# Layer 1's two dense products by Strassen's scheme in a two-layer GraphSAGE kernel

## The reference

```python
def _sage_layer(h, edge_src, edge_dst, deg_inv, W_self, W_neigh, b):
    msg = h[edge_src]
    agg = jax.ops.segment_sum(msg, edge_dst, num_segments=h.shape[0])
    mean = agg * deg_inv[:, None]
    return h @ W_self + mean @ W_neigh + b
h   = jax.nn.relu(_sage_layer(x, src, dst, deg_inv, W_self0, W_neigh0, b0))
out = _sage_layer(h, src, dst, deg_inv, W_self1, W_neigh1, b1)
return _layernorm(x + out, axis=-1)        # x: 1250 x 1024
```

## Time and profile before

| | us |
|---|---|
| median of 3 runs | 683.05 (680.74 to 683.33) |
| the profiled execution, its own time | 681.76 |
| its span, first to last instruction | 680.1 |

### The profile page before, as it was taken

One profiled execution on the slowest core, in us unless ns is written; L12 is line 12 of the kernel. 1 busy time (PEld: TensorE's weight loads), 2 busy tenths in 40 slices (PEclk: granted clock), 3 DMA queues, 4 the chain that ended last, 5 costly groups with the idle time before them and its releaser, 6 DMA issues.

```text
span 680.1 us, 11592 instructions
## 1 busy us (share of the span) xinstructions
PE 646.3 (95%) x3404; PEld 335.0 (49%) x3404; DVE 383.0 (56%) x1003; ACT 198.4 (29%) x349; POOL 118.3 (17%) x194
## 2 busy tenths in 40 slices
PE   3778989998999999999999999999999999999995
PEld 3634545543666666555555444444444444444442
DVE  7796586868777877378889845241033322322223
ACT  5672724344344444213336401231100000000000
POOL 4001236632233333200000000000041111101100
PEclk9799989999999999999999999999999999999999
DMA  8614000000000000060000500000211011111100
GB/s 320 248 70 178 1 0 0 0 0 1 1 1 1 0 0 0 3 249 1 0 0 0 212 36 1 0 0 0 94 63 62 32 62 62 62 62 34 51 31 24
DMA packets 11393, 33.40 MB, mean 49 GB/s; under 512 B 1976, under 2 KB 2136, under 8 KB 11360
## 3 DMA queue, kind: packets, MB, share of 16 engines
q1 hardware_dynamic: 11360, 32.99, 13.2%
HBM read 27.87 MB, written 5.12 MB: 49 GB/s over the span
## 4 chain that ended last, share of the span: by engine, by line
PE 88%; DVE 4%; issue 3%; DMA 2%; ACT 1%; SPq 1%; POOL 0%; POOLq 0%; DVEq 0%; ACTq 0%
PE ps L539 26%; PE ps L653 15%; PE ps L566 15%; PE ps L674 13%; PE ps L605 12%; PE ps L463 5%; DMA ws<-in_L_gnn_W_neigh 2%; DVE wn L248 1%; PE ps L619 1%; SPq L284 1%; DVE xz L967 1%; PE ps L475 1%; DVE ws L248 1%; PE ps L491 1%; ACT ws L726 1%
## 5 line engine op out<-in xcount | busy, mean ns | idle before, releaser
L539 PE MATMUL ps<-wn,xz 128*128 128x512 f16 x480 | 116.5, 382 | 2.8 <-DVE wn L248 1.4
L566 PE MATMUL ps<-xz,ws 128*128 128x420 f16 (+1 forms) x576 | 116.1, 339 | 0.0
L653 PE MATMUL ps<-wn,zh 128*128 128x512 f16 x480 | 105.2, 379 | 0.0
L934 DVE TENSOR_SCALAR scratch<-iota_q,table 125x240 f16<-125x240 f16 x320 | 104.0, 325 | 0.3 <-issue 0.2
L539 PE MATMUL ps<-ws,zh 128*128 128x512 f16 x480 | 103.8, 379 | 0.0
L932 DVE TENSOR_SCALAR lohot<-iota_lo,table 125x128 f16<-125x128 f16 x320 | 87.6, 274 | 26.0 <-PE ps L463 25.2
L380 POOL TENSOR_TENSOR A<-A,scratch 128x120 int32 x160 | 72.6, 454 | 139.5 <-ACT scratch L699 111.5
L699 ACT ACTIVATE scratch<-ps 128x240 uint16<-128x240 f32 x160 | 58.9, 370 | 120.8 <-PE ps L463 102.8
L674 PE MATMUL ps<-xz,A 128*128 128x512 f16 x400 | 88.0, 379 | 0.0
L605 PE MATMUL ps<-A,zh 128*128 128x420 f16 (+1 forms) x480 | 84.7, 340 | 0.0
L653 PEld LDWEIGHTS ps<-wn,zh 128*128 (+1 forms) x480 | 46.9, 98 | 56.7 <-issue 0.2
(11 more groups left out here) (127 smaller groups left out, 432.4 us busy)
## 6 DMA issues: line engine op xcount, KB each, us to landing
ws<-in_L_gnn_W_neigh SPq DMA_DIRECT2D x8, 1024.0 KB, 12.9
zh<-in_x SPq DMA_DIRECT2D x9, 512.0 KB, 8.2
ws<-in_x SPq DMA_DIRECT2D x9, 512.0 KB, 3.2
out<-ws SPq DMA_DIRECT2D x18, 256.0 KB, 2.1
ws<-in_L_gnn_W_self SPq DMA_DIRECT2D x4, 1024.0 KB, 8.7
wn<-in_L_gnn_W_self SPq DMA_DIRECT2D x4, 1024.0 KB, 8.1
ws<-in_L_gnn_b SPq DMA_DIRECT2D x1, 512.0 KB, 3.8
zh<-in_x SPq DMA_DIRECT2D x1, 392.0 KB
```

Source lines behind the costliest of these rows:

```text
L539: ins = pe.matmul(ps[0:TP, 2 * r + half, :], lhs(a, k, t), w[:, k, b, half * HD:(half + 1) * HD], start=(k == 0 and a == 0 and b == 0), st ...
L566: ins = pe.matmul(ps[:, b, 0:CH[n]], ws[:, k, a, bass.ds(f * P, P)], xT[h][:, k, CO[n]:CO[n] + CH[n]], start=(k == 0 and a == 0 and h == 0 ...
L653: ins = pe.matmul(ps[0:TP, g + half, :], zh[:, k, a, bass.ds(t * TP, TP)], wn[:, k, b, half * HD:(half + 1) * HD], start=(k == 0 and a == ...
L934: ins = dve.tensor_scalar(qhot[0:EP, r, k, :], iota_q[0:EP, :], q[0:EP, b, bass.ds(row, 1)], None, ALU.is_equal)
```

## The change

Both dense products of layer 1 are computed by Strassen's scheme (Winograd's form). h is cut in two along the nodes (tile p and tile p+5) and in two along the features (k-tiles 0 to 3 and 4 to 7), the weights in two by two blocks. Each pair p of node tiles then takes seven products m of 12 matmuls of 512 columns (4 k-tiles x 3 splits), where the scheme before took 2 x 48: 35 products or 420 matmuls for each of `h Wn1` and `h Ws1`, not 480.

- h is kept in fp32 (`H`), and no longer split as a whole. Before each product an *item* is made: ACT writes the high part of its operand into a ring of 8 slots, DVE the low part, seven products ahead. Products 5, 6, 3 and 7 of each pair need a sum of two blocks of h, which POOL makes (`s_sum`, chained: each waits for the one before).
- The weights are loaded in pieces, twice (once for their maximum, once for the factors). For each of four k the seven factors T are made: four by subtractions on POOL (`t_sum4`), high parts on ACT, low parts on DVE (28 of each per product stage).
- In the first product stage three products of each pair (1, 5, 6) are copied from PSUM by ACT (`kept`), three (2, 3, 7) are added to such a copy by DVE (`c_made`), and four results of 512 columns are split into z1. In the last one DVE adds each of the 35 products to y in SBUF.
- The two branches of layer 1 are turned round: the first product stage (`h Wn1`), then all ten tiles of `A z1`, whose results with x and b1 added are spilled to DRAM for eight of the ten tiles and read back, then the second product stage (`h Ws1`) with the layer norm in it.
- All of this is written out, where it was in loops.

The core of the diff:

```diff
+    ORDER7 = [(0, 1)]
+    for pair in range(IT):
+        last = pair == IT - 1
+        ORDER7 += [(pair, m) for m in ((5, 6, 3, 7, 2) if last else (2, 5, 6, 3, 7))]
+        ORDER7 += [(pair, 4)] if last else [(pair + 1, 1), (pair, 4)]
...
@@ POOL
             spread(2)
+            for k in range(HK):
+                t_sum4(0, k)
             pool.wait_ge(unit_ready, 3 * (KT - 1))
-            pool.memset(zh[:, 0:KT, :, N:NP], 0.0).then_inc(h_tail_zero, 1)
+            for k in range(KT):
+                ins = pool.memset(H[k][:, N:NP], 0.0)
+            ins.then_inc(h_tail_zero, 1)
+            pool.wait_ge(h32_ready, 3 * KT)
+            for i in range(4):
+                s_sum(i)
             spread(3)
+            for i in range(4, 4 * IT):
+                s_sum(i)
+            pool.wait_ge(b1_in, 16)
+            for n in range(4):
+                residual(n)
             spread(4)
-            pool.wait_ge(b1_in, 16)
-            with pool.Fori(0, IT) as i:
-                residual(i)
+            pool.wait_ge(item_low, NP7)
+            for k in range(HK):
+                residual(4 + k)
+                t_sum4(1, k)
...
+            for i in range(4 * IT, 8 * IT):
+                s_sum(i)
@@ PE
+            def product(phase, e):
+                p, m = ORDER7[e]
+                b = 3 * (p % 2) + {1: 0, 6: 0, 7: 0, 4: 0, 2: 1, 5: 2, 3: 2}[m]
+                pe.wait_ge(item_low, NP7 * phase + e + 1)
+                if phase == 0:
+                    if m == 1 and p >= 2:
+                        pe.wait_ge(z_low, 4 * (p - 1))
+                    if m in (6, 3, 7):
+                        pe.wait_ge(kept_ready, KEEP7.index((p, {6: 1, 3: 5, 7: 6}[m])) + 1)
+                    if m == 4:
+                        pe.wait_ge(c_made, MADE3.index((p, 7)) + 1)
+                else:
+                    if m == 1 and p >= 2:
+                        pe.wait_ge(y_acc, AT7[p - 2, 4] + 1)
+                    if m in (6, 3, 7, 4):
+                        pe.wait_ge(y_acc, AT7[p, {6: 1, 3: 5, 7: 6, 4: 7}[m]] + 1)
...
+                for k in range(HK):
                     for a, bs in ((0, (0, 1)), (1, (0,))):
+                        for w in bs:
+                            ins = pe.matmul(ps[:, b, :], slot[:, k, a, :], Tm[m][:, k, w, :], ...)
...
@@ ACT, first product stage
+            for e in range(1, ITEMS):
+                item(0, e)
+            for e in range(NP7):
+                p, m = ORDER7[e]
+                if e + ITEMS < NP7:
+                    item(0, e + ITEMS)
+                if m in (1, 5, 6):
+                    act.wait_ge(product_done, e + 1)
+                    if p:
+                        act.wait_ge(c_made, MADE3.index((p - 1, {1: 2, 5: 7, 6: 3}[m])) + 1)
+                    act.activation(kept[{1: 0, 5: 1, 6: 2}[m]], ..., ACT.Copy).then_inc(kept_ready, 1)
+                else:
+                    z_item(MADE7.index((p, m)))
@@ DVE, end of the neighbours and last product stage
+                    unit(f, n)
                     if 3 * f + n:
+                        hmax(*divmod(3 * f + n - 1, 3))
...
+            item_lows(0, 0)
+            hmax(KT - 1, 2)
...
+            for e in range(NP7):
+                p, m = ORDER7[e]
+                if e + ITEMS < NP7:
+                    item_lows(1, e + ITEMS)
...
+                dve.wait_ge(product_done, NP7 + e + 1)
+                dve.scalar_tensor_tensor(yh, ps[0:TP, 3 * (p % 2) + b, :], c("cs1", TP), yh,
+                                         ALU.mult, ALU.add).then_inc(y_acc, 1)
+                if m in (2, 3, 7, 4):
+                    dve.wait_ge(y_acc, e + 1)
+                    dve.bn_stats(st[0:TP, r, 6 * h:6 * h + 6], yh).then_inc(stat_ready, 1)
+                if m == (3 if p < IT - 1 else 2):
+                    finish(2 * p)
+                if m == 4:
+                    finish(2 * p + 1)
```

More of the change, by code:

```diff
@@ L324, in store_row @@
                     apart(sp)
-                    rows = LAST if isinstance(i, int) and 2 * i + r == JT - 1 else TP
-                    sp.dma_start(out[bass.ds((2 * i + r) * TP, rows), half], obuf[r][0:rows, half]).then_inc(o_stored[r], 16)
-            def tile_slices(t):
-                with sp.If(nwin > 1):
-                    load_slices(sp, TILES + t, t * TP, TP)
-            for r in range(2):
-                load_row(0, r, True)
-            for r in range(2):
-                tile_slices(r)
@@ L337, in _ @@
-            with sp.Fori(0, IT - 2) as i:
-                for r in range(2):
-                    load_row(i + 1, r)
-                    store_row(i, r)
-                    tile_slices(2 * i + 2 + r)
-            for r in range(2):
-                load_row(IT - 1, r)
-                store_row(IT - 2, r)
-                tile_slices(2 * IT - 2 + r)
-            for r in range(2):
-                store_row(IT - 1, r)
+                    sp.dma_start(out[t * TP:t * TP + rows, half], yrow(p, r)[0:rows, half]).then_inc(o_stored[r], 16)
@@ L662, in tile @@
+            for e in range(NP7):
+                product(0, e)
+            def tile(n, with_rest):
+                t = TILES_B[n]
+                g = 6 if n % 2 == 0 else 3
+                if n >= 2:
+                    pe.wait_ge(y_ready, 2 * n - 2)
+                elif n == 1 or with_rest:
+                    pe.wait_ge(z_low, 4 * IT)
+                if n == 0 and not with_rest:
+                    pe.wait_ge(z_low, 4 * (IT - 1))
                 if with_rest:
                     for j in range(JT):
-                        w = slice_in(pe, TILES + t, j)
+                        w = slice_in(pe, TILES + n, j)
@@ L840, in finish @@
+            act.wait_ge(scale_ready, 6)
+            for k in range(HK):
+                for i in range(ITEMS):
+                    t_item(1, k, i)
+            act.wait_ge(t_low, 2 * ITEMS * HK)
+            for e in range(ITEMS):
+                item(1, e)
+            def finish(n):
+                p, r = n // 2, n % 2
+                y = yrow(p, r)
+                act.wait_ge(var_ready, n + 1)
                 act.activation(ln[0:TP, r, 1:2], ln[0:TP, r, 0:1], ACT.Sqrt).then_inc(std_ready, 1)
-                act.wait_ge(shift_ready, t + 1)
@@ L842, in finish @@
-                if not first:
-                    act.wait_ge(o_stored[r], 32 * i)
-                act.activation(obuf[r][:, 0:HD], ybuf[r][:, 0:HD], ACT.Identity, bias=ln[0:TP, r, 3:4],
+                act.wait_ge(shift_ready, n + 1)
+                act.activation(y[:, 0:HD], y[:, 0:HD], ACT.Identity, bias=ln[0:TP, r, 3:4],
                                scale=ln[0:TP, r, 2:3]).then_inc(o_ready[0], 1)
-            finish(0, 0, True)
-            finish(0, 1, True)
-            with act.Fori(1, IT) as i:
-                for r in range(2):
-                    finish(i, r, False)
+            for e in range(NP7):
+                p, m = ORDER7[e]
+                if e + ITEMS < NP7:
+                    item(1, e + ITEMS)
+                if m == (3 if p < IT - 1 else 2):
+                    finish(2 * p)
+                if m == 4:
+                    finish(2 * p + 1)
@@ L1086, in _ @@
                 onehots(NG - GT + g, g, (NG - GT + g) // GR)
-            def groups(i, extra):
-                for r in range(2):
-                    if not (isinstance(i, int) and i == 0 and r == 0):
-                        low(2 * i + r - 1, 1 - r, 1)
-                    for m in range(2):
-                        extra(i, 2 * r + m)
             nwin = dve.value_load(nwin_i[0:1, 0:1], min_val=1, max_val=NWIN)
@@ new lines, in _, with z_low_part @@
+            for e in range(1, ITEMS):
+                item_lows(0, e)
+            def z_low_part(i):
+                p, m = MADE7[i]
+                t, half = p + (IT if m in (7, 4) else 0), slice(0, HD) if m in (2, 4) else slice(HD, D)
+                dve.wait_ge(z_high, i + 1)
+                dve.scalar_tensor_tensor(z1[1][:, t, half], ps[:, 3 * (p % 2), :] if m == 4 else
+                                         made[MADE3.index((p, m)) % 2], c("s_z1"), z1[0][:, t, half],
+                                         ALU.mult, ALU.subtract).then_inc(z_low, 1)
```

566 lines of the change are left out of this document (367 added, 199 removed).

## The result

The changed kernel took **703.66 us** (median of four runs, 702.37 to 704.27) beside 682.92 for the kernel before: a ratio of 1.0308, 95% interval 1.0281 to 1.0334. The forecast was 678 us, faster, with a range up to 690: wrong in sign, and outside its range. The profiled execution has a span of 702.2 us, against 680.1 before and 675.1 by the forecast's sum: 27.1 us are to be explained. Of the runs further down, e8 had two slow executions among its ten (840.53 and 1322.84 us): its median of 683.41 counts them, its ratio leaves them out.

A forecast was written before the change was run, and what follows sets the result against it. PE was taken to bound the kernel, busy 95% of the span. -25.9 + 2.4 + 10.4 + 1.5 + 4.2 + 0.9 + 1.5 = -5.0 us, so 683.05 - 5.0 = 678 us, range 665 to 690.

The forecast's parts named there:

- What it removes: Both dense products of layer 1: 60 of 480 matmuls fewer in each, at 0.2158 us, 25.9 us saved.
- Neighbours: Neighbours stage: DVE about 74 of 84.3 us, no loss taken; slack of 10 us as cover, up to 5 if POOL is late.
- Start of the first product: Start of first product stage: PE waits 2.4 us for item 0's low part, on DVE behind the last unit.
- The fifth sum: First product stage: POOL's fifth item sum, behind `spread(3)` and its two operation changes, makes PE wait 10.4 us.
- Clock: First product stage: granted clock 0.50 for 3 us, expected once, behind the long wait; 1.5 us lost.
- Tiles: Tiles stage: POOL 65.5 of 86.3 us, DVE about 47; nothing lost, up to 4 us if the POOL chain comes late.
- Last product: Last product stage: DVE's queue makes PE wait 0.4 and 0.8 us at products 3 and 4 of pairs; 4.2 us.
- POOL against DVE: DVE low parts slowed beside POOL's sums: 1.5 us taken, between nothing and 24 us for a stage.
- Rival 2: Last product stage bound by DVE, low parts waiting 0.4 us behind each of 20 sums; 6 to 7 us added, 685; chance 0.17.
- signs of being wrong: Layer 1: idle before the neighbours end, a last stage of over 100 us, or a long wait on the items themselves.

The follow-up runs named there:

- e8: e7 with the sixteen differences of the first factor (neighbours stage) on DVE too, so POOL reads nothing there; 683.41 us.
- e10: Changed kernel rearranged: no spread on POOL, factor differences and first four item sums on DVE, row maxima replaced by ACT's absolute sums, low parts four ahead; 667.40 us.
- e1: Changed kernel with each of POOL's 76 sums and differences replaced by three writes of a constant, sums left out of the computation; 25.5 us less.
- e9: e4 with each of POOL's 76 sums replaced by three writes of a constant, sums left out of the computation; 673.06 us.
- e4: e3 with the maxima of both second factors also spread off POOL, so POOL changes no operation in the part the change touches; 689.08 us.
- e3: Changed kernel with the maximum of h spread by a diagonal on DVE, a product with ones on PE and a DVE reduction, not on POOL; 6.8 us less.
- e2: e1 with one write of a constant in place of three, so POOL neither reads SBUF nor takes long; 10.4 us less than e1.
- e7: e6 with one maximum per row of h instead of three, and last-stage low parts after the running product's accumulation and statistics; 683.34 us.
- e5: Changed kernel with low parts of items 3 to 6 of the last product stage moved after the last tile's eviction on DVE; 703.48 us.
- e6: e4 with e5's move, and the first four item sums of each product stage made by DVE instead of POOL; 686.84 us.

## Why the prediction was wrong

- **What it removes, 25.9 us:** right. The last product of e10 takes 91.0 us for 420 matmuls.
- **Neighbours, "I take nothing":** wrong in the changed kernel, with the cover named (DVE's slack of 10 us), and right without the blocking: in e1 the stage and the wait behind it take 87.1 us, forecast 86.7. DVE's own work was estimated at 74 us; without blocking it is 77.9 to 80.9 (e1 over 84.7 us, e9), and blocking brings it to 89.3 of 92.6 in e4.
- **Start of the first product, 2.4 us:** the mechanism and size are right once nobody blocks DVE (2.44 in e1 and e9). With blocking it is 5.68.
- **The fifth sum, 10.4 us:** measured 10.24, in the place and with the two changes as forecast: 6.03 us of idle time ahead of the spread and 7.36 behind it, against 5.77 and 6.95 of the earlier trace rows. That the size fits so well is partly luck. Counted from the end of the neighbours (383.23), h was complete after 5.2 us and not after 2.1, and the fifth sum ended after 26.7 and not 21.9; but PE too had its four products done only after 17.9 and not 12.8, by the longer wait for item 0 and the low clock behind it. And it was not 10.4 us to be had: behind it lay the next wait, and e3 got 6.8.
- **Clock, 1.5 us:** the first product has a granted clock of 0.94, and it fell twice, behind either long wait, not once. Product 1 took 4.24 us to the start of the next and product 3 took 4.96, where 2.59 is the pace: 4.0 us in all. These are the 2.5 us that the stage is over its forecast.
- **Tiles, "nothing, by up to 4 us":** the second failed step. I had listed `spread(4)` with its changes and compared POOL's sum of 65.5 us with the 86.3 us of the stage. The chain x, residual, factor sums, low parts is serial through POOL and DVE, and the change at `spread(4)` in its middle (9.47 us of idle time on POOL ahead of it, 7.41 behind) made it late: 12.8 us lost, of which e3 and e4 gave back 9.7 and e9 another 2.6.
- **Last product, 4.2 us:** right, mechanism and size. From 609 us on five waits on `L1513` are 3.5 us together: 0.61 before product 3 of pair 0, where none was forecast, and 0.61 to 0.76 before product 4 of pairs 0 to 3. Before product 3 of pairs 1 to 3 the record has 0.12 us of idle time each, and product 6 takes 2.88 us to the start of 3 instead of 2.59. e2, with POOL's writes short, has hardly more than those before products 3 and 4 and takes 94.8 us for the stage, forecast 94.9; e7 removed them by order alone. The stage of the changed kernel is 5.9 us longer than forecast, mostly by a wait of 3.02 us before product 6 of pair 0 and by 1.7 us of low clock behind the wait for item 0.
- **POOL against DVE, 1.5 us:** the step that failed. Its upper bound stood in the text at 24 us for one stage; I chose near the lower, because "neither critical path of mine has a low part right behind a sum but at the start". The measured size is 15.5 us (e9 against e4) over four stages. Rival 2 priced it for the last stage alone. The argument looked for a low part on a path that I had drawn beforehand; but every blocked low part lengthens DVE's queue, and in the neighbours and at both starts that queue was the path. All three signs of being wrong that the prediction names came: idle time before the neighbours end (2.4 us), a last stage of over 100 us (100.8), long waits on the items (9.0).

Together: 15.1 us of span for the changes at the spreads, of which I had counted 11.9, and 15.5 for the blocking, of which I had counted 1.5. That the first pair lies so close is luck as well: the 11.9 were all put on `spread(3)`, which gave 7.0 of span, and nothing on `spread(4)`, which with `spread(2)` gave 8.1. e9, with neither, stands at 673.1, against 683.05 - 25.9 + 2.4 + 4.2 + 0.9 = 664.7 by the same sum. The remaining 8.4 us (9.8 by the profiled spans) are for the most part neighbours (89.3 against 86.7, of which 1.7 are the wait for the new diagonal), first product (94.1 against 90.7) and last product (97.3 against 94.9). e2 shows what much of the last two is: with POOL's writes a third as long they take 92.3 and 94.8 us, so POOL's own length is worth some 2 us in either. The rest was not taken apart; and that the neighbours in e10 still take 88.4 us with 76.1 of DVE's work in 86.8 is open too. That PE's two branches are turned round was not tried by itself.

## What to carry to other kernels

Before work is put on POOL beside a busy DVE, count the DVE instructions with two SBUF inputs that run beside its reading ones, and add to DVE's load for them, everywhere and not only on the path drawn beforehand. POOL's time is the upper bound; here its 76 sums, 1.27 to 1.6 us each, cost DVE 37 us, half a microsecond for each, of which 15.5 reached PE; then ask whether that load still fits the stage. A saving on PE is only worth what the slowest feeding queue leaves: here 25.9 us of matmuls bought nothing until the feed was rearranged, and then 16 (e10). When one wait is removed, look for the one right behind it before counting its length as gain.

## What the hardware showed unexpectedly

- `partition_all_reduce` between writes of a constant on POOL stood without a gap (e1, 388.73 to 389.57); between additions in layer 1 (the changed kernel, e1, e2, e3, e5) 5.7 to 9.5 us of idle time lay ahead of it and 6.9 to 7.5 behind. Why `spread(4)` has 9.4 us ahead of it and `spread(3)` 6.0 is open.
- Small DVE instructions are longer beside POOL's sums as well: in e10 three products of single columns took 1.86 us (0.55 in e6, with POOL idle), and a multiplication of 128x10 by a column 1.33 (0.23 in e6).

```profile
398.82 1.86 DVE L1291 SCALAR_TENSOR_TENSOR S<-S 128x1 f32<-128x1 f32 x3
400.71 1.33 DVE L1505 TENSOR_SCALAR dinvT<-dinvT,S 128x10 f32<-128x10 f32 x1
```
